# Second half of the MLP with the weight blocks stationary, evacuated as columns and transposed back to rows

## The chip, the cores and the metric

The kernel runs on one core of one Trainium2 chip. The time is device microseconds of one launch, from the chip. Everything is float32.

## What is computed

The reference is two layers over x (16 sequences of 112 rows, 512 wide) and a context (16 x 375 x 512): a cross-attention block with an MLP, then a recurrent block. Cut to what matters here:

```
# layer 0, x: (16, 112, 512), ctx: (16, 375, 512)
hidden = softmax(mask(q @ k.T * scale)) @ v @ cproj_w + cproj_b + x      # q from layer_norm(x), k, v from ctx, 16 heads
y = layer_norm(hidden, ln2_w, ln2_b)
y = gelu(y @ fc_w + fc_b, approximate=True)      # fc_w: 512 x 2048
y = y @ proj_w + proj_b                          # proj_w: 2048 x 512   <- the change
x = hidden + y
# layer 1, recurrent, 32 heads of 16:
xa = ln(x); sx = shifted(xa) - xa                # mixes, low-rank products, projections r, k, v, g
s = k v^T + w * s                                # scan over the 112 rows
x1 = x + group_norm(out) * g @ Wo.T
return x1 + sigmoid(xr2 @ Wfr.T) * (relu(xk2 @ Wfk.T)**2 @ Wfv.T)
```

## The kernel before

The 16 sequences are worked in four groups g = 0..3 of four sequences b (`GB = 4`, `T = GB * LQ = 448` columns). All engines run programs written out by hand, with semaphores between them; nothing is scheduled by a planner. For each group TensorE (PE) runs: the attention steps of its four sequences; `mlp(g)`; `border(g)`; `pre(g)` (the first mixes and projections of the recurrent layer). The recurrence of group p = g - 1 runs on VectorE (DVE), cut into `scan_unit`s of some 2 us that are laid between DVE's attention work of group g, and what is left of them is done during `mlp(g)`. After group 3 a last stage runs its scan and the second half of layer 1. "Rows" means that the 112 sequence positions lie on the partitions and the 512 channels along the free axis; "columns" means 128 channels on the partitions (four such blocks e) and 448 positions along the free axis.

`mlp(g)` takes the 2048 hidden channels in four pieces m. A piece is 16 products of `fc` (channels on the partitions, 448 positions moving, weight block stationary; ScalarE (ACT) applies gelu into `HT`, line 1150) and then 16 products of `pj` (line 533): stationary is `HT[:, c, b]` (128 x 112), moving is the weight row block `w[:, c, :]` (512 wide), and the output is rows, one PSUM bank of `SC` = (2, 3, 4, 5) for each sequence b, accumulated over all 16 blocks (m, c). With the last c of the last m the tiles `("ACC", g, b)` are closed one after another. The trace has two TensorE instructions for each of these matmuls, and one for each transpose.

PSUM has eight banks; a bank can be opened again when its last tile is freed by the engine that reads it. `WIDE` = (0, 1, 6, 7) is taken in turn by the `fc` products and, in `border`, by the transposes `pre_cols` and the products `recurrence_out`. Weights come through `ring`, two slots of 1 MB, filled by SyncE (SP) in the order of use, each when the piece before last is over.

What follows the MLP, in `border(g)`:

- DVE: `mlp_add(g, b)` (X += bank, line 1534, then the layer-norm statistics, lines 1312 and 1314), GpSimd (POOL) makes 1/std (lines 868, 871), DVE `pre_apply(g, b)` (line 1540).
- PE: for g = 0 only `pre_cols(g, 0..3)` (line 368, four transposes each), each waiting for its `pre_apply`. For g > 0: `recurrence_out` 0 and 1 (the output projection Wo of group g - 1, 8 instructions each of 512 columns, out of `C[0]`, which waits for `og_ready`), `pre_cols` 0 and 1, `recurrence_out` 2, `pre_cols` 2 and 3, `recurrence_out` 3. DVE adds each to X (line 1546).
- ACT turns the four `("LN", "pre", g, b)` tiles into `XA` (line 1057), DVE makes the shifted difference and the mixes (lines 1462 to 1457), and PE begins `pre(g)` (line 611).

`og_ready` comes at the end of a chain on DVE: scan of p done, `group_norm(p)` (its square root is on ACT, line 1167, behind gelu number (3, 0) in ACT's program), y out to DRAM and back in another layout (SP, `y_columns`), `gate(g)` (lines 1520 and 1523).

`mlp_bias(g)` (line 1528) adds `proj_b`, spread over the rows in `pb`, to X: one DVE instruction of 112 x 2048 for each group, before DVE's remaining scan units. `pb` is loaded at the start by ACT's queue (line 1026), one of 13 loads that ACT issues before its first activation; TensorE and DVE wait for 11 of them as `PARAMS`.

`C[1]` (128 x 4 x 448) is a work buffer: the scan of group p keeps its state in it (`S_mid`) and `pre(g)` its mixes.

## Time and profile before

| | |
|---|---|
| median of 3 runs | 1761.23 us (1757.83 to 1768.81) |
| the profiled execution, its time | 1756.24 us |
| its span in the trace | 1753.9 us |
| TensorE busy | 1638.1 us, 93% |
| VectorE busy | 1188.7 us, 68% |
| ScalarE busy | 657.4 us, 37% |
| GpSimd busy | 281.6 us, 16% |
| granted TensorE clock, mean | 0.975 |

The trace numbers are from one profiled execution. "Busy" counts an instruction from start to end; TensorE instructions overlap, so the pace of a stream of them is read from start to start and not from the duration of one. The chain that ended last is followed back from the last instruction; a wait is listed in square brackets behind the row that waited, with the engine and tile that ended it.

### The profile page before, as it was taken

The numbers are of one execution on the slowest core, as the hardware profiler recorded it, in microseconds if no ns is written. First come the engines' busy times: TensorE is split into PE (matmuls) and PEld (weight loads), VectorE is DVE, ScalarE is ACT, GpSimd is POOL, SyncE is SP. The second block draws the span as 40 slices with busy tenths as digits, with TensorE's granted clock in tenths as the row PEclk, the third lists the DMA queues.
The fourth block names the chain that finished last, engine by engine and source line by source line (L and its number), as shares of the span: only waits on it lengthen the run. The fifth ranks groups of instructions, "written<-read, shape, count | busy, mean of one in ns | idle before, by whom it ended". The sixth has DMA issues, their size and how long they took to land.

```text
span 1753.9 us, 21083 instructions
## 1 busy us (share of the span) xinstructions
PE 1638.1 (93%) x7912; PEld 855.8 (49%) x7912; DVE 1188.7 (68%) x1854; ACT 657.4 (37%) x1535; POOL 281.6 (16%) x377
## 2 busy tenths in 40 slices
PE   6999999799999999899999998999899898987968
PEld 3555544455555444455554445555444454433423
DVE  1233200367997995569988955799899576999741
ACT  2466420226664212246662222466431226212111
POOL 1100000123111001322110011221100132036020
PEclk9999999899999999999999999999999998999989
DMA  8001012143121124341112233510132343232221
GB/s 272 6 30 53 19 48 80 68 138 99 38 61 50 64 84 143 102 135 46 38 59 75 76 129 96 161 46 9 47 101 83 117 115 111 64 105 77 69 90 45
DMA packets 76914, 142.46 MB, mean 81 GB/s; under 512 B 16688, under 2 KB 26800, under 8 KB 76816
## 3 DMA queue, kind: packets, MB, share of 16 engines
q1 hardware_dynamic: 61664, 105.51, 18.9%
q0 software_dynamic: 11776, 31.70, 6.4%
q10 hardware_dynamic: 3376, 3.93, 0.7%
q8 instruction: 64, 1.05, 0.2%
q14 instruction: 34, 0.28, 0.1%
HBM read 117.26 MB, written 23.86 MB: 80 GB/s over the span
## 4 chain that ended last, share of the span: by engine, by line
PE 74%; DVE 16%; issue 4%; ACT 3%; ACTq 1%; DMA 1%; POOL 0%; DVEq 0%; POOLq 0%
PE bank L346 42%; PE bank L533 12%; PE bank L660 7%; PE bank L388 4%; DVE C L1399 3%; PE bank L380 3%; PE bank L400 2%; DVE sm L1336 1%; PE bank L626 1%; DVE C L1575 1%; DVE C L1391 1%; PE bank L611 1%; DVE SX L1399 1%; DVE C L1408 1%; DVE YB L1417 1%
## 5 line engine op out<-in xcount | busy, mean ns | idle before, releaser
L1399 DVE TENSOR_TENSOR_SCAN C<-XA,C 128x896 f32<-128x896 f32 x112 | 228.8, 2043 | 3.7 <-ACT XA L1091 0.5
L533 PE MATMUL bank<-ring,HT 128*112 128x512 f32 x512 | 222.3, 592 | 0.0
L1336 DVE CUSTOM_DVE_ANT_0 sm<-bank,maskb 112x375 f32<-112x375 f32 x256 | 124.3, 543 | 133.6 <-PE bank L380 133.1
L346 PE MATMUL bank<-ctx_t,Wk 128*128 128x375 f32 x512 | 195.2, 506 | 13.9 <-DMA Wk<-in_wk 12.5
L346 PE MATMUL bank<-SX,ring 128*128 128x448 f32 (+2 forms) x544 | 195.9, 519 | 4.1 <-issue 4.1
L346 PE MATMUL bank<-Wv,ctx_t 128*125 128x512 f32 x384 | 180.9, 596 | 0.4 <-ACT C L1057 0.4
L388 PEld LDWEIGHTS bank<-ident,sm 112*125 112x125 f32 x768 | 124.1, 190 | 105.6 <-ACT sm L1072 44.1
L1078 ACT ACTIVATE probT<-bank 125x336 f32<-125x336 f32 x256 | 114.3, 446 | 159.3 <-PE bank L388 157.6
L1072 ACT ACTIVATE sm<-sm,nm 112x375 f32<-112x375 f32 x256 | 153.4, 599 | 2.7 <-DVE nm L1336 2.7
L533 PEld LDWEIGHTS bank<-ring,HT 128*112 128x112 f32 x512 | 90.6, 177 | 127.2 <-issue 127.2
L346 PEld LDWEIGHTS bank<-SX,ring 128*128 128x128 f32 x544 | 100.5, 190 | 96.9 <-issue 94.0
L1150 ACT ACTIVATE HT<-bank,colt 128x448 f32<-128x448 f32 x64 | 40.5, 634 | 257.6 <-PE bank L346 257.5
L388 PE MATMUL bank<-ident,sm 112*125 112x112 f32 x768 | 125.4, 272 | 9.0 <-ACT probT L1078 8.9
L346 PEld LDWEIGHTS bank<-ctx_t,Wk 128*128 128x128 f32 x512 | 90.5, 196 | 62.2 <-issue 28.2
L1391 DVE TENSOR_TENSOR C<-VB,rkw 128x1776 f32<-128x1776 f32 x56 | 112.3, 2005 | 8.4 <-DMA VB<-v_scratch 4.1
L660 PE MATMUL bank<-C,ring 128*128 128x448 f32 x256 | 107.2, 569 | 10.3 <-DVE C L1590 7.7
L1091 ACT ACTIVATE XA<-rkw 128x896 f32<-128x896 f32 x64 | 60.9, 952 | 130.3 <-DVE C L1408 47.7
L1408 DVE TENSOR_TENSOR C<-C,rkw 128x1792 f32<-128x1792 f32 x53 | 107.3, 2025 | 1.8
L868 POOL TENSOR_SCALAR vare_ln<-mv_ln 112x1 f32<-112x1 f32 x32 | 21.9, 686 | 467.5 <-DVE mv_ln L1314 467.5
L1417 DVE TENSOR_TENSOR YB<-YB,C 128x1792 f32<-128x1792 f32 x45 | 91.0, 2022 | 1.2
L346 PEld LDWEIGHTS bank<-Wv,ctx_t 128*125 128x125 f32 x384 | 65.0, 188 | 49.4 <-issue 49.4
L1534 DVE TENSOR_TENSOR X<-bank,X 112x512 f32<-112x512 f32 x16 | 10.9, 680 | 108.8 <-PE bank L533 108.7
(181 smaller groups left out, 2317.1 us busy)
## 6 DMA issues: line engine op xcount, KB each, us to landing
ring<-in_stream SPq DMA_DIRECT2D x64, 1024.0 KB, 5.4
ctx_t<-in_ctxT SPq DMA_DIRECT2D x16, 750.0 KB, 4.7
rkw_scratch<-HT POOLq DMA_DIRECT2D x32, 224.0 KB, 4.3
rkw<-rkw_scratch POOLq DMA_DIRECT2D x24, 224.0 KB, 3.1
HT<-in_x SPq DMA_DIRECT2D x16, 224.0 KB, 5.2
X<-in_x SPq DMA_DIRECT2D x16, 224.0 KB, 5.1
rkw_scratch<-YB POOLq DMA_DIRECT2D x16, 224.0 KB, 3.1
v_scratch<-HT POOLq DMA_DIRECT2D x16, 224.0 KB, 5.6
```

The lines of the kernel that those rows point to most:

```text
L346: last_ = nc.tensor.matmul(out_ap, pairs[k][0], pairs[k][1], start=(k == 0), stop=(k == len(pairs) - 1))
L388: last_ = nc.tensor.transpose(bank[k][0:KW, c * LQ:(c + 1) * LQ], sm[0:LQ, slot, c * KW:(c + 1) * KW], ident[0:LQ, 0:LQ])
L533: last_ = nc.tensor.matmul(bank[SC[b]][0:LQ, :], HT[:, c, b * LQ:(b + 1) * LQ], w[:, c, :], start=(m == 0 and c == 0), stop=(m == 3 and c ...
L660: last_ = nc.tensor.matmul(bank[k[e]][:, 0:T], w[:, c, e * P:(e + 1) * P], mixed[at][:, c, :], start=(c == 0), stop=(c == E - 1))
L1072: nc.scalar.activation(sm[0:LQ, slot, :], sm[0:LQ, slot, :], ACT.Exp, bias=nm[:, slot:slot + 1], scale=-1.0, accum_out=den[:, n % 2, e * H ...
L1078: nc.scalar.activation(probT[:, r, :], tile(name)[0:KW, 0:KC * LQ], ACT.Copy).then_inc(freed(name), 1)
L1091: nc.scalar.activation(wrep[:, i % 2, :].rearrange("p (j t) -> p j t", j=JH), rkw[:, (i // BLOCK) % 2, i % BLOCK, 2, :].unsqueeze(1).to_br ...
L1336: nc.vector.tensor_tensor_reduce(out=sm[0:LQ, slot, :], in0=tile(name)[0:LQ, 0:LK], in1=maskb[:, n % 2, :], scale=-SCALE, scalar=3.0e38, o ...
L1391: own.step(nc.vector.tensor_tensor(S[:, :, 1:LQ], VB[:, :, 0:LQ - 1], kk[:, 0:LQ - 1].unsqueeze(1).to_broadcast([P, RS, LQ - 1]), ALU.mult))
L1399: own.step(nc.vector.tensor_tensor_scan(out=part, data0=wrep[:, i % 2, :], data1=part, initial=0.0, op0=ALU.mult, op1=ALU.add))
L1408: prod = nc.vector.tensor_tensor((S if last or i > 0 else YB)[:, :, :], S[:, :, :], r.unsqueeze(1).to_broadcast([P, RS, LQ]), ALU.mult)
L1417: nc.vector.tensor_tensor(YB[:, :, :], YB[:, :, :], S[:, :, :], ALU.add).then_inc(scan_step, 1)
```

## The change

For the `pj` pieces the operands change places. The weight block `w[:, c, e*128:(e+1)*128]` (128 x 128) is now stationary and all 448 columns of `HT[:, c, :]` move; the output is columns, one bank of `SC` for each channel block e. For m < 3 the order is c outside, e inside, as before with b. For m = 3 it is e outside and c inside, so that the four output tiles close one after another, 4 products apart. ACT evacuates each with the bias `proj_b` as a per-partition value into `C[1][:, e, :]` (new function `mlp_out`; it waits for the end of the scan of group p, since that uses `C[1]`). PE transposes each back into rows (new function `mlp_rows`: 4 sequences, each 128 x 112 stationary against a 128 x 128 identity), one e behind the products, into the four `WIDE` banks; these are the new tiles `("AT", g, b)`, and `mlp_add` reads them in place of `ACC`. `mlp_bias`, `pb` and its load are gone; `proj_b` is 4 more columns of `colt`. In `border` for g > 0 the tiles of `pre_cols` and `recurrence_out` get fixed banks in place of the turn, and `any_first` starts with `WIDE` from its first bank.

```diff
-                    for c in range(E):
-                        evacuated(pe, ("FC", g, 4 * m + c))
-                        for b in range(GB):
-                            if m == 0 and c == 0:
-                                opened(SC[b])
-                            last_ = nc.tensor.matmul(bank[SC[b]][0:LQ, :], HT[:, c, b * LQ:(b + 1) * LQ], w[:, c, :],
-                                                     start=(m == 0 and c == 0), stop=(m == 3 and c == E - 1))
-                            if m == 3 and c == E - 1:
-                                closed(last_, ("ACC", g, b), SC[b])
+                    if m < 3:
+                        for c in range(E):
+                            evacuated(pe, ("FC", g, 4 * m + c))
+                            for e in range(E):
+                                if m == 0 and c == 0:
+                                    opened(SC[e])
+                                last_ = nc.tensor.matmul(bank[SC[e]][:, 0:T], w[:, c, e * P:(e + 1) * P], HT[:, c, :],
+                                                         start=(m == 0 and c == 0), stop=False)
+                    else:
+                        for e in range(E):
+                            for c in range(E):
+                                evacuated(pe, ("FC", g, 4 * m + c))
+                                last_ = nc.tensor.matmul(bank[SC[e]][:, 0:T], w[:, c, e * P:(e + 1) * P], HT[:, c, :],
+                                                         start=False, stop=(c == E - 1))
+                            closed(last_, ("ACC", g, e), SC[e])
+                            if e > 0:
+                                mlp_rows(g, e - 1)
+                        mlp_rows(g, E - 1)
...
+            def mlp_rows(g, e):
+                evacuated(pe, ("ACC", g, e))
+                for b in range(GB):
+                    if e == 0:
+                        opened(WIDE[b])
+                    last_ = nc.tensor.transpose(bank[WIDE[b]][0:LQ, e * P:(e + 1) * P],
+                                                C[1][:, e, b * LQ:(b + 1) * LQ], ident[:, :])
+                    if e == E - 1:
+                        closed(last_, ("AT", g, b), WIDE[b])
...
             def pre_cols(g, b):
-                k = wide()
+                k = opened((SC[2], SC[3], WIDE[1], WIDE[2])[b])
             def recurrence_out(g, w, b):
-                k = wide()
+                k = opened((SC[0], SC[1], WIDE[0], WIDE[3])[b]) if g < NG else wide()
...
-            act.dma_start(pb[:, :], proj_b.partition_broadcast(LQ)).then_inc(params_in, 16)
...
+            def mlp_out(g):
+                if g > 0:
+                    act.wait_ge(scan_step, g * RS)
+                for e in range(E):
+                    name = ("ACC", g, e)
+                    ready(act, name)
+                    nc.scalar.activation(C[1][:, e, :], tile(name)[:, 0:T], ACT.Identity, bias=col("proj_b", e)
+                                         ).then_inc(freed(name), 1)
...
             def mlp_add(g, b):
-                name, rows = ("ACC", g, b), rows_of(g, b)
+                name, rows = ("AT", g, b), rows_of(g, b)
...
-                    mlp_bias(g)
```

TensorE at the end of `mlp(1)` and in `border(1)`, before (the last four of the 16 `pj` products, then the border; `ring,C0` are the products of Wo, `ident,xn` and `ident,GT` the transposes of `pre_cols`):

```order
L533 MATMUL bank2<-ring,HT 112x512
L533 MATMUL bank3<-ring,HT 112x512
L533 MATMUL bank4<-ring,HT 112x512
L533 MATMUL bank5<-ring,HT 112x512
L346 MATMUL bank1<-ring,C0 112x512 x4
L346 MATMUL bank6<-ring,C0 112x512 x4
L368 MATMUL bank7<-ident,xn 128x112 x4
L368 MATMUL bank0<-ident,xn 128x112 x4
```

The same place in the changed kernel, from the fourth of the four output tiles of the last piece on (`ident,C1` are the new transposes):

```order
L538 MATMUL bank5<-HT,ring 128x448 x4
L556 MATMUL bank0<-ident,C1 112x128
L556 MATMUL bank1<-ident,C1 112x128
L556 MATMUL bank6<-ident,C1 112x128
L556 MATMUL bank7<-ident,C1 112x128
L556 MATMUL bank0<-ident,C1 112x128
L556 MATMUL bank1<-ident,C1 112x128
L556 MATMUL bank6<-ident,C1 112x128
L556 MATMUL bank7<-ident,C1 112x128
L344 MATMUL bank2<-ring,C0 112x512 x4
L344 MATMUL bank3<-ring,C0 112x512 x4
L366 MATMUL bank4<-ident,xn 128x112 x4
```

Behind the last product stand eight transposes (four for e = 2, then four for e = 3), and only then the first product of Wo; it has moved from bank 1 to bank 2, the first `pre_cols` from bank 7 to bank 4.

ACT's queue at the start, before, from the fourth load on (the loads stand ahead of ACT's first activation):

```order
L1025 DMA Wc<-in_wc 128x4x512
L1026 DMA pb<-in_proj_b 112x512
L1027 DMA mw<-in_maa_w 128x4x160
L1028 DMA mw<-in_maa_w 128x512
L1029 DMA mw2b<-in_maa_w 128x512
```

In the changed kernel the load of `pb` is missing and the others follow in the same order.

## Rows read from the trace of the kernel before

**Rows 1.** Page: busy times; lines of the chain that ended last
```profile
PE 1638.1 (93%) x7912; PEld 855.8 (49%) x7912; DVE 1188.7 (68%) x1854; ACT 657.4 (37%) x1535; POOL 281.6 (16%) x377
PE bank L346 42%; PE bank L533 12%; PE bank L660 7%; PE bank L388 4%; DVE C L1399 3%; PE bank L380 3%; PE bank L400 2%; DVE sm L1336 1%; PE bank L626 1%; DVE C L1575 1%; DVE C L1391 1%; PE bank L611 1%; DVE SX L1399 1%; DVE C L1408 1%; DVE YB L1417 1%
```

**Rows 2.** Table by stretches: from:to and length, busy of each engine, granted clock
```profile
238.90:329.90 91.00, 90.99 (x224) 40.54 (x222) 2.38 (x5) 8.24 (x13) 0.67 (x2) 1.00 0.25 81
329.90:341.20 11.30, 3.23 (x16) 2.12 (x16) 7.58 (x17) 5.71 (x16) 5.28 (x11) 0.69 0.31 104
408.00:559.00 151.00, 149.59 (x997) 87.82 (x997) 140.98 (x234) 99.69 (x263) 31.17 (x30) 1.00 0.16 44
1113.00:1273.80 160.80, 147.20 (x960) 84.97 (x960) 146.94 (x232) 94.40 (x249) 27.31 (x26) 0.97 0.17 50
```

**Rows 3.** Chain in order of time, two pieces of mlp(0): start, length, line
```profile
252.61 12.03 PE bank L346 x32
264.63 13.73 PE bank L533 x32
```

**Rows 4.** Timeline: a pj piece begins behind an fc piece
```profile
290.23 13.90 PE L533 MATMUL bank<-ring,HT 128*112 128x512 f32 x32
290.43 0.63 ACT L1150 ACTIVATE HT<-bank,colt 128x448 f32<-128x448 f32 x1 [2.37 <-PE bank L346]
```

**Rows 5.** Timeline of TensorE in border(1): eight transposes and what follows
```profile
686.91 0.93 PE L368 MATMUL bank<-ident,xn 112*128 112x112 f32 x8
687.68 3.60 PE L346 MATMUL bank<-ring,C 128*112 128x512 f32 x8
```

**Rows 6.** Timeline of border(0), TensorE and the first DVE add
```profile
326.72 3.17 PE L533 MATMUL bank<-ring,HT 128*112 128x512 f32 x7
327.42 0.69 DVE L1534 TENSOR_TENSOR X<-bank,X 112x512 f32<-112x512 f32 x1 [105.13 <-PE bank L533]
331.06 0.61 PE L368 MATMUL bank<-ident,xn 112*128 112x112 f32 x4 [1.17 <-DVE xn L1540]
335.02 1.01 PE L368 MATMUL bank<-ident,GT 112*128 112x112 f32 x4 [1.38 <-DVE GT L1540]
341.23 4.01 PE L611 MATMUL bank<-C,mw 128*32 128x112 f32 x93 [3.89 <-DVE C L1457]
```

**Rows 7.** border(1): DVE's timeline, and the chain's piece of Wo's first products
```profile
673.89 2.03 DVE L1523 TENSOR_TENSOR C<-C,GT 128x1792 f32<-128x1792 f32 x1
680.21 6.87 PE bank L346 x16
682.72 0.52 DVE L1540 TENSOR_SCALAR xn<-X,mv_pre,rstd_pre 112x512 f32<-112x512 f32 x1
687.84 1.04 DVE L1540 TENSOR_SCALAR GT<-X,mv_pre,rstd_pre 112x512 f32<-112x512 f32 x2
```

**Rows 8.** Tile pb; then the gate of mlp(3): ACT, DVE, Wo's products, SP's loads
```profile
L1528 DVE TENSOR_TENSOR X<-X,pb x4: 2293/2293/2294, 220.0 to 1271.6; 112x2048 f32<-112x2048 f32 x4
1358.62 0.39 ACT L1167 ACTIVATE gst<-gst,epsc 128x112 f32<-128x112 f32 x1 [2.13 <-DVE gst L1448]
1372.95 2.02 DVE L1523 TENSOR_TENSOR C<-C,GT 128x1792 f32<-128x1792 f32 x1
L346 PE MATMUL bank<-ring,C x32: 591/592/595, 1377.1 to 1392.0; 128*112 128x512 f32 x32
1367.65 25.29 SPq L774 DMA_DIRECT2D ring<-in_stream  x3
ring<-in_stream SPq DMA_DIRECT2D x1, 1024.0 KB, 6.4
```

**Rows 9.** Timeline of the start: ACT's load of pb, its first activation, TensorE's wait
```profile
2.97 0.55 ACTq L1026 DMA_DIRECT2D pb<-in_proj_b  x1
19.41 1.28 ACT L1040 ACT_TABLE_LOAD   x1 [19.41 <-issue]
21.33 5.32 PE L346 MATMUL bank<-ctx_t,Wk 128*128 128x375 f32 x16 [1.45 <-ACT KT L1040]
```

More of the change, by code:

```diff
@@ L32 @@
         "r_ln1_w", "r_ln1_b", "r_ln2_w", "r_ln2_b", "maa_x",
-        "maa_0", "maa_1", "maa_2", "maa_3", "maa_4", "decay", "gn_w", "gn_b", "mix_k", "mix_r"]
+        "maa_0", "maa_1", "maa_2", "maa_3", "maa_4", "decay", "gn_w", "gn_b", "mix_k", "mix_r", "proj_b"]
 FCB = E * len(COLS)
@@ L117, in close, with build @@
         self.at[name] = (self.done, bank, self.opened[bank])
-def build(nc, x, ctxT, ctx, mask, shiftcols, cols, wq, wk, wv, wc, cproj_b, proj_b, stream,
+def build(nc, x, ctxT, ctx, mask, shiftcols, cols, wq, wk, wv, wc, cproj_b, stream,
           maa_w1, maa_w2, td_w1, td_w2, u, out):
@@ L145, in build @@
         cb = sb("cb", [LQ, D])
-        pb = sb("pb", [LQ, D])
         shc = sb("shc", [P, 2, E, B])
@@ L238, in build @@
         params_in = sem("params_in")
-        PARAMS = 11
+        PARAMS = 10
         consts_made = sem("consts_made")
@@ L329, in any_first @@
             def any_first():
-                first = turn_of["wide"] + 1
-                any_order[:] = [*SC, *(WIDE[(first + k) % 4] for k in range(4))]
+                any_order[:] = [*SC, *WIDE]
                 turn_of["any"] = -1
@@ L1280, in _ @@
                     mlp(g)
+                    mlp_out(g)
                     pre_cols(g)
@@ L1523, in gate @@
                 nc.vector.tensor_tensor(C[0][:, :, :], C[0][:, :, :], GT[:, :, :], ALU.mult).then_inc(og_ready, 1)
-            def mlp_bias(g):
-                rows = X[:, (g % 2) * GB:(g % 2 + 1) * GB, :]
-                dve.wait_ge(xn_ready["ln2"], g * GB + GB)
-                own.step(nc.vector.tensor_tensor(rows, rows, pb[:, :].unsqueeze(1).to_broadcast([LQ, GB, D]), ALU.add))
-                own.settle()
             def mlp_add(g, b):
-                name, rows = ("ACC", g, b), rows_of(g, b)
+                name, rows = ("AT", g, b), rows_of(g, b)
                 ready(dve, name)
@@ L1711 @@
             *[l1["maa_stack"][0, j] for j in range(5)], l1["time_decay"], l1["gn_w"], l1["gn_b"],
-            l1["ffn_maa_k"], l1["ffn_maa_r"], l0["fc_b"]]
+            l1["ffn_maa_k"], l1["ffn_maa_r"], l0["proj_b"], l0["fc_b"]]
     cols = np.concatenate([v.reshape(-1, P).T for v in vecs], axis=1)
@@ L1729 @@
         "wq": l0["q_w"], "wk": l0["k_w"], "wv": l0["v_w"], "wc": l0["cproj_w"],
-        "cproj_b": l0["cproj_b"], "proj_b": l0["proj_b"],
+        "cproj_b": l0["cproj_b"],
         "stream": np.stack(pieces),
```

## The prediction

> **What bounds the kernel now.** I read the page first: TensorE is busy 93% of the span, and of the chain that ended last the two matmul lines 346 and 533 alone are 54%; line 533, the second half of the MLP, is 12% of it [rows 1]. Then the table by stretches. Between 238.9 and 329.9 us (fc and pj of group 0) TensorE is busy the whole time at full granted clock, and DVE does 2.4 us of work: the MLP is TensorE's alone. Right behind it, 329.9 to 341.2 us, TensorE has 3.2 us of work in 11.3 us and waits for DVE, ACT and GpSimd in turn; this is border(0), and it is on the chain too [rows 2]. In group 3's attention (1113 to 1273.8 us) TensorE and DVE are both at 147 us of 160.8: there DVE leads [rows 2]. But its work begins only when pre(2) has produced its inputs, so a gain made upstream moves this stretch and doesn't shrink in it. The same holds for the final scan. So the end moves by the sum of what the four MLPs, the four borders behind them and the start give.
>
> **The products.** The chain has an fc piece (32 instructions of 448 columns) at 12.03 us and a pj piece (32 of 512 columns) at 13.73 us [rows 3]. After the change a pj piece has exactly the shape of an fc piece: 128 x 128 stationary, 448 moving. So 1.70 us for each of 4 pieces in 4 groups: 6.80 us a group, 27.2 us in all. The stationary block grows from 112 to 128 columns; the fc piece has that already, so 12.03 us includes it.
>
> **The transposes.** 16 a group, each 128 columns of the identity. Before, eight transposes of 112 columns go from 686.91 to 687.68 us, 0.096 us each, with products right before and behind them [rows 5]; scaled to 128 columns 0.11 us. That is 1.76 us a group, 7.0 us in all. The upper bound is the same instruction at the lower clock level: four take 1.01 us at 335.02 us against 0.61 us at 331.06 [rows 6], which with the drain taken off is about twice, 0.2 us each, 6 us more in all. Nothing suggests a price under 0.096.
>
> **The wait for the last tile.** ACT must evacuate tile e = 3 before its four transposes. The fc tiles show this latency: the next piece's first product starts at 290.23 us, ACT starts on the tile just closed at 290.43 and takes 0.63 us [rows 4]. With 0.05 us to wake TensorE that is 0.88 us, of which 0.44 us lie under the four transposes of e = 2; then 0.44 us for those of e = 3. So from the last product to the first product of Wo: 1.32 us. The other eight transposes stand between products, 0.88 us. Net for TensorE's own stream: 6.80 - 0.88 - 1.32 = 4.60 us a group.
>
> **Border(0).** Here TensorE has nothing to cover DVE's chain, and the chain's start moves the other way: before, tile b = 0 closes three tiles ahead of the end, and DVE's first add starts at 327.42, 2.30 us before the last product has issued (326.72 + 3.17 less 0.16 of drain, 329.73) [rows 6]. After, no row tile is whole until the transposes of e = 3: 0.88 + 0.11 + 0.15 (drain) = 1.14 us behind the last product. The products end 6.80 - 0.88 = 5.92 us earlier, the add is 1.14 + 2.30 = 3.44 us later against them: border(0) gains 2.48 us, not 4.60. This is the step where the change gives back most.
>
> **Borders 1 to 3.** There 6.87 us of Wo products stand before the first `pre_cols` [rows 7]. DVE's chain starts some 2.4 us later against them. Before, `pre_apply` of b = 1 is done at 683.24, 3.2 us after Wo's products began (about 680.05) and 3.7 before the transposes at 686.91; 2.4 later is still in time. `pre_apply` of b = 2, 3 is done at 688.88 [rows 7], while their transposes come at about 691.1 (687.68 + 8 x 0.43) [rows 5]; DVE's queue has slack there from waits on Wo's tiles, and by my count the second apply then ends some 1.3 us before it is needed. So nothing is lost, and the fixed banks add no wait: bank 2 to 5 are freed by ACT's four evacuations, before Wo's first product may start at all.
>
> **The gate.** Wo's products also need `og_ready`. In group 1 it comes at 675.92 [rows 7], about 4.1 us ahead of 680.05; 4.60 us would close it. But `mlp_bias`, 2.29 us of DVE ahead of the scan's rest, is gone [rows 8], and ACT reaches the square root 5.1 us (three pieces) earlier, for which DVE waited; so the gate moves by about 5 us with the products. Group 3 is tight: the square root there already waits for DVE (2.13 us), so only the 2.29 us count. og_ready goes from 1374.97 to 1372.68, the products from 1377.10 [rows 8] to 1372.50: a wait of 0.23 us. Wo's weights, issued by SP behind y at 1367.65 and 6.4 us on the way [rows 8], go the same 2.29 us earlier, to 1371.8, in time by 0.7. ACT stays blocked behind the square root until about 1358.0, and gelu 1 to 3 follow at 0.6 us each, just ahead of the products that read them. `mlp_out`'s wait for the scan's end is long over: that comes some 15 us before the gate. ACT's four evacuations lie in its idle time. Group 3 gains 4.37 us, groups 1 and 2 4.60 each.
>
> **The start.** ACT issues its 13 loads until 19.4 us, then loads its table, and only the first evacuation lets TensorE go on at 21.33, after 1.45 us of waiting [rows 9]. The issue of `pb` is 0.55 us of that, and the later issues stand in a full queue with 224 KB less ahead. Between 0 and the 1.45 us of the wait; I take 0.8.
>
> **Sum.** 2.48 + 4.60 + 4.60 + 4.37 + 0.8 = 16.85 us. Against the profiled execution, 1756.24 us: 1739.4. That execution was 5 us under the median of the three runs, 1761.23, whose range is 11 us; against that: 1744.4. I predict 1742.5, between the two.
>
> **The rivals.**
>
> A, the gain is smaller because it is taken off the path. (1) The transposes cost twice, 6 us more: a gain of 11. (2) The gate doesn't move with the products: in each of three groups Wo then starts when it starts now less what bias gives, 2.3 us instead of 4.6: 7 us less, a gain of 10. Either gives about 1749. For it speaks the tight gate in group 3; against it that DVE's idle time before the square root in groups 1 and 2 is itself due to TensorE.
>
> The Trainium skill, "TensorE: Matmul & The Clock Gate", part 4, gives about 275 ns for a 128 x 128 transpose in a kernel's context, bf16. By that the 64 new ones are 17.6 us and the change would gain about 6 us. The eight transposes that take 0.77 us in this trace speak against it as a pace; it would be a latency.
>
> B, slower than before: the clock. If TensorE fell to its lower level (1.2 GHz) at the run of eight transposes with a wait in it, and stayed there over the border, the 32 instructions of Wo (13.7 us at full clock) would take 13.7 us more, in three groups 41 us: about 1780. It is slower than before from two of the three borders on. In this trace the clock fell only in border(0), mean 0.69, after TensorE had been idle more than half of 5 us, and was 1.00 in the attention of group 1, which is full of short transposes [rows 2]. The new wait is 0.44 us. The same page, part 4, says that transposes don't engage the full clock; the attention stretch speaks against that here.
>
> C, more than I count: ACT's queue at the start frees TensorE by the full 1.45 us, and border stretches at the lower clock get shorter. Another 2 us, 1740.5.
>
> **The numbers.** My forecast with C: 0.78. A: 0.18. B: 0.04. 1% of 1761.23 is 17.6 us, about what a measurement of this kernel can tell from no change, and my sum is 16.85: it lies on that bound, and chance decides most. The median of three before lies above its profiled execution, which tilts it a little to faster. Faster by over 1%: 0.50; within 1%: 0.46; slower: 0.04, which is B. The range: 1734 (C, with a median as low as the profiled execution) to 1752 (A, with the spread of medians).
>
> **What would show it.** In the changed profile: 12.03 us a pj piece for m < 3; the last product to Wo's first 1.3 us; new transposes at 0.11 us; the first add of border(0) at about 324.9 less what the start gave; the stretch from the first product of pj (0) to Wo shorter by 4.6 us in groups 1 to 3, with at most some tenths waited for line 1523 in group 3; granted clock 1.00 in borders 1 to 3; TensorE's first wait for ACT at 0.7 us. It is wrong if the transposes are slower than 0.15 us, if `pre_cols` waits for `pre_apply` in groups 1 to 3, or if stretches outside MLP and border change length by more than a microsecond in sum.

## The result and the profile after

The changed kernel takes 1737.49 us (median of four runs, 1736.41 to 1739.64); the kernel before, measured again beside it, 1762.68 (1757.83 to 1768.81). The ratio is 0.986, with an interval of 0.984 to 0.988: faster by 1.4%. I had forecast 1742.5, in a range of 1734 to 1752. Run a second time, the changed kernel took 1739.02 us, ratio 0.985 (0.983 to 0.988). Its profiled execution is one of 1739.64 us with a span of 1736.7.

Line numbers are a little different in the new kernel: 344 is the old 346, pj is 532 (m < 3) and 538 (m = 3) instead of 533, the transposes back are 556, the first products of `pre` are 629 instead of 611. First the page's busy times and the lines of the chain that ended last (answer to [rows 1]). TensorE has 16 us less to do, and stays 93% busy: it is the bound as before.

```profile
PE 1621.9 (93%) x7976; PEld 870.2 (50%) x7976; DVE 1178.6 (68%) x1850; ACT 666.3 (38%) x1551; POOL 281.0 (16%) x377
PE bank L344 40%; PE bank L678 8%; PE bank L532 6%; DVE C L1426 5%; PE bank L386 4%; PE bank L378 3%; PE bank L538 2%; PE bank L398 2%; DVE C L1435 2%; DVE YB L1444 2%; DVE sm L1363 1%; DVE C L1596 1%; DVE C L1418 1%; PE bank L644 1%; PE bank L629 1%
```

Pieces of the chain in mlp(0) (start, length, line): a pj piece now costs what an fc piece costs, as against [rows 3]. The third row is half a piece, the part of m = 3 up to the first transposes.

```profile
239.63 12.03 PE bank L532 x32
251.65 12.03 PE bank L344 x32
311.79 6.01 PE bank L538 x16
```

The table by stretches, with the columns of [rows 2]: MLP of group 0 from pj (0), then border(0), then the first part of border(1). TensorE fills the MLP, and the granted clock is full (1.00, the level of 2.4 GHz) there and in border(1).

```profile
239.50:325.40 85.90, 85.63 (x237) 43.59 (x235) 0.00 (x0) 10.76 (x17) 0.00 (x0) 1.00 0.26 86
325.40:339.58 14.18, 4.28 (x20) 2.81 (x21) 9.98 (x21) 5.69 (x16) 5.93 (x12) 0.68 0.27 83
677.80:694.60 16.80, 15.46 (x50) 6.97 (x48) 11.91 (x24) 5.58 (x16) 5.22 (x11) 1.00 0.33 107
```

Since the granted clock differs a little from one execution to the next, spans alone don't say where the time went. So I cut every trace at TensorE's own milestones: the first pj product of group g ("pj"), and the first product of `pre(g)` (the row that answers to the last of [rows 6]). Lengths in us; "before again" and "after again" are the two kernels unchanged, run and profiled a second time.

| stretch | before | after | before again | after again |
|---|---|---|---|---|
| start to pj(0) | 238.71 | 239.46 | 240.16 | 241.31 |
| pj(0) to pre(0) | 102.52 | 100.12 | 102.52 | 100.12 |
| pre(0) to pj(1) | 247.80 | 251.80 | 247.81 | 248.28 |
| pj(1) to pre(1) | 107.84 | 103.26 | 107.84 | 103.26 |
| pre(1) to pj(2) | 249.71 | 247.57 | 249.48 | 246.90 |
| pj(2) to pre(2) | 107.84 | 103.26 | 107.84 | 103.26 |
| pre(2) to pj(3) | 231.66 | 229.68 | 231.93 | 229.64 |
| pj(3) to pre(3) | 107.84 | 104.17 | 107.83 | 104.33 |
| pre(3) to the end | 360.00 | 357.38 | 363.28 | 359.49 |

The four changed stretches repeat to 0.2 us and give 2.40 + 4.58 + 4.58 + 3.67 = 15.23 us. The others should be equal, and aren't: they differ by between -2.6 and +4.0 us in the first pair, and between -3.8 and +1.2 in the second. The two spans differ by 17.2 and 22.1 us.

### The profile page after: what moved, and what is told of

It reads as the page before. It is cut to its first block, busy times and chain, and to the rows that moved or that the text cites. A ratio compares the mean times of both kernels' runs of the same rounds, so it can differ in the third digit from the quotient of the medians.

```text
span 1736.7 us, 21228 instructions
## 1 busy us (share of the span) xinstructions
PE 1621.9 (93%) x7976; PEld 870.2 (50%) x7976; DVE 1178.6 (68%) x1850; ACT 666.3 (38%) x1551; POOL 281.0 (16%) x377
## 3 DMA queue, kind: packets, MB, share of 16 engines
q8 instruction: 64, 1.05, 0.3%
## 4 chain that ended last, share of the span: by engine, by line
PE 69%; DVE 21%; issue 5%; ACT 3%; ACTq 1%; DMA 1%; POOL 0%; SPq 0%; DVEq 0%; POOLq 0%
PE bank L344 40%; PE bank L678 8%; PE bank L532 6%; DVE C L1426 5%; PE bank L386 4%; PE bank L378 3%; PE bank L538 2%; PE bank L398 2%; DVE C L1435 2%; DVE YB L1444 2%; DVE sm L1363 1%; DVE C L1596 1%; DVE C L1418 1%; PE bank L644 1%; PE bank L629 1%
## 5 line engine op out<-in xcount | busy, mean ns | idle before, releaser
L532 PE MATMUL bank<-HT,ring 128*128 128x448 f32 x384 | 146.3, 539 | 0.0
L532 PEld LDWEIGHTS bank<-HT,ring 128*128 128x128 f32 x384 | 73.0, 190 | 71.4 <-issue 71.4
```

What stands on the lines that cost most here:

```text
L532: last_ = nc.tensor.matmul(bank[SC[e]][:, 0:T], w[:, c, e * P:(e + 1) * P], HT[:, c, :], start=(m == 0 and c == 0), stop=False)
```

## Experiments

Two theories stood against the rest. Mine: a change of this kind is worth its terms on TensorE's stream (products, transposes, one evacuation's wait). The rivals: transposes cost their recorded duration or pull down the clock; the bias instruction that left DVE brings the gain; and, for what lies outside the MLP, that it is the random clock, against something the change moved.

**The two kernels, unchanged, side by side** (no edit).

> The kernel before once more with a profile, beside the others of this call. Its first profiled execution took 1756.24 us, 5 to 7 us under its medians. Theory 1 (the difference is clock and start, outside MLP and border): MLP and border repeat (102.5 us in group 0 from the first pj product to pre's first, 107.84 in groups 1 to 3), and the spare microseconds stand in the stretches outside with a lower granted clock. Theory 2 (the profiled execution was typical and the medians of before are high for another reason): the new profile is again within 1 us of 1753.9.

> The changed kernel once more, beside the others of this call. The stretches fixed by the program (first pj product to the first product of pre) should repeat to 0.05 us: 99.95, 103.09, 103.10 and 104.17 us for groups 0 to 3. Theory 1 (the 7 us between the change in medians and the change in spans, 24.5 against 17.2, come from stretches outside MLP and border in which the granted clock falls at other moments): the stretches outside differ between two profiles of one kernel by microseconds of either sign, and the granted clock of these stretches with them. Theory 2 (the change moves work outside MLP and border for good): they repeat to some tenths.

Measured: 1761.56 us for the kernel before (0.999, 0.998 to 1.001) and 1739.02 for the changed one. The table has their stretches. The MLP and border stretches are the same in both pairs, so they are the change's; so are three of the others, by sign: pre(1) to pj(2), pre(2) to pj(3) and pre(3) to the end are shorter by 1.98 to 3.79 us in both pairs. That needed a cause of its own (below). The two traces of the kernel before differ by 4.8 us, nearly all of it ahead of pj(0) and behind pre(3); I had expected lower granted clocks there, but the longer one has the higher mean clock (0.976 against 0.975), so this difference stays open.

**Every transpose back twice.**

```diff
-                    last_ = nc.tensor.transpose(bank[WIDE[b]][0:LQ, e * P:(e + 1) * P], ...
+                    for again in range(2):
+                        last_ = nc.tensor.transpose(bank[WIDE[b]][0:LQ, e * P:(e + 1) * P], ...
```

> Each of the 64 new transposes is issued twice. Theory (0.109 us each, those of e = 2 lie under the wait for ACT as far as it goes, 0.44 us): each MLP is 12 x 0.109 longer where nothing covers (e = 0, 1 and 3) and the four more of e = 2 fill the wait of 0.44 us, so 1.31 us a group from the first pj product to the first product of Wo, 5.2 us in all; in group 3, where Wo waits 0.7 us for its weights, 0.6. Rival (a transpose costs about 275 ns on the path, the Trainium skill's figure in TensorE: Matmul & The Clock Gate, part 4): 3.3 us a group and more. Rival on the clock: the granted clock in borders 1 to 3 falls below 1.00 with 20 transposes in a row.

Measured: 1739.62 us (0.986, 0.983 to 0.989); pj to Wo 87.75 us in groups 1 and 2 (86.44 without), so 1.31 more, and 0.45 more in group 3, where I had expected 0.6. The median doesn't show the 5.2 us that I expected in all: it lies 2.1 and 0.6 us above the two medians of the changed kernel, and its four runs are spread over 7.9 us (1735.03 to 1742.92). Only the stretches show the price. Sixteen records of it in a row, from the timeline of border(1), and the group by lines (min, median and max duration in ns):

```profile
678.46 1.97 PE L557 MATMUL bank<-ident,C 128*112 128x128 f32 x16
680.27 4.03 PE L344 MATMUL bank<-ring,C 128*112 128x512 f32 x9
L557 PE MATMUL bank<-ident,C x128: 272/273/322, 317.9 to 1364.4; 128*112 128x128 f32 x128
```

Sixteen take 1.81 us, 0.11 each, and the record of one says 272 ns. So the recorded duration is how long one takes from entering to leaving, and the next enters after 0.11: a sum over durations would have been 2.5 times too high. The granted clock stayed at 1.00 in borders 1 to 3. The Trainium skill, "TensorE: Matmul & The Clock Gate", part 4, gives about 275 ns for a 128 x 128 transpose in bf16 within a kernel, and says that transposes don't bring the full clock; its figure agrees with the duration here (273 ns, in float32) and not with the pace, and its warning had no effect in a border that is mostly products.

**Transposes all at the end, and a simpler order of products.** `tail` does the four rounds of transposes only after the last product of m = 3. `couter` does that and also runs piece m = 3 in the order of the others.

```diff
 (tail)
                             closed(last_, ("ACC", g, e), SC[e])
-                            if e > 0:
-                                mlp_rows(g, e - 1)
-                        mlp_rows(g, E - 1)
+                        for e in range(E):
+                            mlp_rows(g, e)
 (couter, besides)
-                    if m < 3:
...
-                    else:
+                    for c in range(E):
+                        evacuated(pe, ("FC", g, 4 * m + c))
                         for e in range(E):
...
+                                                     start=(m == 0 and c == 0), stop=(m == 3 and c == E - 1))
+                            if m == 3 and c == E - 1:
+                                closed(last_, ("ACC", g, e), SC[e])
```

> The changed kernel with all 16 transposes of a group behind the last product. Theory: the last tile's evacuation (0.88 us) is then covered by twelve transposes (1.31 us) and not by four, TensorE's wait of 0.29 to 0.44 us goes: 0.44 us a group less up to the first product of Wo, so 99.5 us in group 0 and 102.65 in groups 1 and 2, 104.17 unchanged in group 3, where weights and gate bind; 1.3 us in all, too little for the medians. Rival: sixteen transposes in a row cost more each than four between products (0.11), or take the granted clock down behind them; then groups 1 and 2 are above 103.1 us.

> tail with c outside and e inside for the last piece too (the same loop as for the first three), so that the four column tiles close 0.75 us apart at the end and not 3.0. Theory: ACT's evacuations (0.63 us each) keep pace with tiles 0.75 us apart, and the sixteen transposes start before the last tile is needed: 99.6, 102.76, 102.76 us from the first pj product to pre's first in groups 0 to 2, as in tail to 0.1 us. The e order of the last piece is then without effect once the transposes are at the end. Rival: TensorE waits for the first tiles, and it is longer by up to 0.6 us a group.

Measured: `tail` 1732.99 us (0.982, 0.980 to 0.985), `couter` 1732.13 us (0.982, 0.980 to 0.985). pj to Wo is 85.93 in both, in groups 1 and 2, 0.51 less than in the changed kernel. The timeline of `tail` in border(1):

```profile
670.77 1.91 PE L555 MATMUL bank<-ident,C 128*112 128x128 f32 x16
672.52 7.03 PE L344 MATMUL bank<-ring,C 128*112 128x512 f32 x16
```

Sixteen transposes in 1.75 us without a gap: ACT's evacuation of tile 3 lies under the twelve transposes of tiles 0 to 2. The order c or e outermost makes no difference, so the code of the change that turned it for m = 3 isn't needed. In group 3 they gain little or nothing (87.33 and 87.06 against 87.30): Wo's first product waits there 1.2 and 1.0 us, until DVE's multiplication ends. 0.5 us in each of three groups is not the 4.5 to 5.4 us by which their medians lie under 1737.49. In the two traces much of the rest is clock: it stayed at 1.00 from 54 to 74 us, where the changed kernel's fell to 0.71, and start to pj(0) took 236.3 and 236.1 us against 239.5. But all eight runs of the two (1734.91 at most) lie below the eight of the changed kernel (1734.93 at least), and why the clock should favour them isn't shown.

**Only the operands changed, no way back.** The tiles of 448 columns are added to 448 columns of the rows as they are, without ACT's evacuation, `mlp_out` or transposes; the bias and the way back to rows are left out. A first version, `products`, took the turn-taking banks in border, and kept the changed bank order of `pre`; the second put that order back.

```diff
 (products; the loops of the products as in couter, without mlp_rows)
-                    mlp_out(g)
...
-                k = opened((SC[2], SC[3], WIDE[1], WIDE[2])[b])
+                k = wide()
...
-                k = opened((SC[0], SC[1], WIDE[0], WIDE[3])[b]) if g < NG else wide()
+                k = wide()
...
-                name, rows = ("AT", g, b), rows_of(g, b)
+                name, rows = ("ACC", g, b), rows_of(g, b)
 (products2, besides)
-                any_order[:] = [*SC, *WIDE]
+                first = turn_of["wide"] + 1
+                any_order[:] = [*SC, *(WIDE[(first + k) % 4] for k in range(4))]
```

> The changed operands of the products alone: 448 columns moving, but c outside and e inside for all four pieces, no evacuation into C[1], no transposes; DVE adds the column tiles to X as they are, so that proj_b and the way back to rows are left out. Theory: against the kernel before, each pj piece 12.03 instead of 13.73 us; from the first pj product to the first product of Wo 6.80 us shorter in groups 1 and 2 (103.1 becomes about 100.9), in group 0 border and MLP 6.5 us shorter (about 95.9 instead of 102.35 us); in group 3 the gate stands at the same place, so no shorter than the changed kernel's 104.17 us by more than 0.1 us. Span about 8 us under the changed kernel's, apart from what the clock does outside. Rival (the gate or pre_cols take the gain): groups 1 and 2 stay above 102 us.

> As products (operands changed alone, proj_b and the way back to rows left out), but with the order of banks in pre as in the kernel before: any_first begins behind the bank that the turn has reached. In products the fifth tile of pre's first product stood on bank 0, which held the last Wo tile; TensorE waited 4.98 us there for DVE's add. Theory: from Wo's first product to pre's first 16.83 us again in groups 1 and 2 (20.4 in products), so 101.0 us from the first pj product; group 3 at 104.3 (gate); group 0 unchanged at 95.7. Rival: the wait in products came from something else and stays.

Measured: `products` 1741.34 us (0.986, 0.982 to 0.990), `products2` 1733.99 (0.984, 0.982 to 0.987). pj to Wo is 84.19 in both, 6.82 less than 91.01: the term for the operands alone (6.80) to 0.02. But Wo to `pre` took 20.4 us in `products`, where 16.8 is usual. The first line is its timeline in border(1):

```profile
686.15 6.07 PE L620 MATMUL bank<-C,mw 128*32 128x112 f32 x128 [4.98 <-DVE X L1558]
685.19 0.68 DVE L1558 TENSOR_TENSOR X<-bank,X 112x512 f32<-112x512 f32 x1
```

`pre`'s fifth tile fell on the bank that held the last Wo tile, and TensorE stood 5 us until DVE had read it. I hadn't foreseen that wait; with the order of banks put back, pj to pre is 101.02, as expected. It also shows that the banks of border and the order in which `pre` opens them belong together: the change turned both, and to turn one alone costs 3.6 us a border (104.6 against 101.0). Group 3 came out at 102.17 instead of 104.3: DVE's multiplication ended 85.2 us behind the first pj product, where the changed kernel has 87.2. The stretch pre(2) to pj(3), in which DVE scans, had been 2.1 us longer (231.7 against 229.7).

**The bias back on DVE.** `mlp_bias` as before, at its old place, with `cb` as the operand (2.29 us of DVE in each group).

```diff
                     y_apply(n)
+                    mlp_bias(g)
...
+                own.step(nc.vector.tensor_tensor(rows, rows, cb[:, :].unsqueeze(1).to_broadcast([LQ, GB, D]), ALU.add))
```

> The changed kernel with one DVE instruction of 112 x 2048 back in the place of mlp_bias, adding cb (already on chip) in place of pb, so that the output has a wrong bias and the load at the start stays away. Theory: DVE's chain to og_ready in group 3 is 2.29 us later and Wo waits that much longer, 89.6 us from first pj product to Wo instead of 87.3; groups 1 and 2 have room of 5.1 us and stay at 86.44; group 0 stays. Rival A2 (the gate binds in groups 1 and 2 as well): these move too.

Measured: 1740.65 us (0.988, 0.987 to 0.990); pj to pre 103.27 in groups 1 and 2, unchanged, and 105.85 in group 3, 1.7 more than 104.17. So what left DVE brought nothing where TensorE sets the end, and 1.6 to 1.7 us in the one group in which the gate is tight. The full 2.29 don't arrive, because DVE's wait for y took up part of it: DVE's last write of y came 2.1 us later, but it then waited 9.06 us for y where it had waited 9.61, so the multiplication ended 1.6 us later (88.8 against 87.2 us behind the first pj product; in the kernel before, 88.9). The chain in `gate`'s timeline of group 3:

```profile
1359.16 1.78 DVE L1547 TENSOR_SCALAR C<-C,colt 128x448 f32<-128x448 f32 x4 [9.06 <-DMA C<-y_scratch]
1360.97 2.03 DVE L1550 TENSOR_TENSOR C<-C,GT 128x1792 f32<-128x1792 f32 x1
1363.16 3.26 PE L344 MATMUL bank<-ring,C 128*112 128x512 f32 x7 [0.21 <-DMA ring<-in_stream]
```

**The load of `pb` back.**

```diff
+        pb = sb("pb", [LQ, D])
...
-        PARAMS = 10
+        PARAMS = 11
...
+            act.dma_start(pb[:, :], proj_b.partition_broadcast(LQ)).then_inc(params_in, 16)
```

> The changed kernel with the load of pb kept at its old place in ACT's queue and nothing reading it. Theory: ACT's first activation comes 0.8 us later again (19.4 instead of 18.6 us), and TensorE's third key product at 21.3 instead of 20.54 us; TensorE starts its first product at 12.5 instead of 11.3 us; all stretches of MLP and border as in the changed kernel. Rival C (the start gives nothing or the full 1.45 us).

Measured: 1738.65 us (0.987, 0.985 to 0.989), so nothing that a time can show against 1737.49 and 1739.02. In the trace, ACT's table load begins at 19.42 and the third key product at 21.34 us, as before ([rows 9]: 19.41 and 21.33), against 18.62 and 20.54 without the load. TensorE's own first product was expected at 12.5 us again and came at 11.11 (11.26 in the changed kernel), so that part was a miss. The load of `pb` doesn't set it: the second trace of the kernel before, which has the load, begins at 11.20.

```profile
19.42 1.28 ACT L1059 ACT_TABLE_LOAD   x1 [19.42 <-PE bank L345]
21.34 1.85 PE L345 MATMUL bank<-ctx_t,Wk 128*128 128x375 f32 x5 [2.14 <-ACT KT L1059]
```

This run also had no wait at Wo in group 3 (86.44, as in groups 1 and 2): its attention of group 3 was 3.8 us longer, at a mean granted clock of 0.96 against 0.97, and y went out 1.7 us earlier against the first pj product. A longer attention leaves DVE more time ahead of the gate, and its length differs from one execution to the next. That isn't the whole rule: `couter`, whose attention of group 3 was 2.2 us shorter, waited no longer for it.

**The kernel before, its instructions moved.** Sixteen transposes that nobody reads, ahead of the first fc product of each group: 32 instructions, weight loads included, and 1.75 us each. It tells whether the shorter stretches behind the borders come from where the instructions lie.

```diff
                     evacuated(pe, ("TY", g * GB + b))
+                for again in range(16):
+                    nc.tensor.transpose(bank[first][:, 0:P], ident[:, :], ident[:, :])
```

> The kernel before with 16 more transposes of the identity in each group, at the start of mlp(g), into a bank that the next product overwrites: TensorE's program is as much longer before each border as in the changed kernel, and nothing else is touched. Before, TensorE stops for 1.86, 1.26 and 1.46 us in the middle of pre's first product (line 611) in borders 1 to 3, with nothing that it waits for; in the changed kernel these stops are gone, and in products2, which has the changed products but no transposes, they are there (1.67, 1.12, 1.82). Theory F (the stops come when TensorE's next 16 KB of instructions are late, and their place in the program decides): no stop of over 0.4 us in line 611 in groups 1 to 3; from pre's first product to the next pj product about 2 us less the 1.75 us that the added transposes take (they lie in this stretch): 249.7 becomes 249.5, 231.7 becomes 231.5; pj to pre unchanged at 107.84. Theory G (the changed banks of pre took the stops away): they stay at 1.3 to 1.9 us, and the stretches are 251.4 and 233.4 us.

Measured: 1769.96 us (1.003, 1.001 to 1.005), some 6 us more (2 to 10), where 64 transposes take 7.0. pj to pre stayed at 107.84. Theory F, that the place in the program decides, holds for groups 1 and 3 (no stop; pre(1) to pj(2) 249.18 us, expected 249.5) and missed group 2, where a stop of 2.63 us was left (236.11 us, expected 231.5). G falls, since the banks are those of the kernel before. What follows from its trace stands in the last section.

**A version that should beat all.** `tail`, and the gate by blocks: each e of `C[0]` is multiplied at once and raises `og_ready`, Wo's first tile waits block by block, and SP issues Wo's weights ahead of y's last two loads.

```diff
+                    for e in range(E):
+                        own.step(nc.vector.tensor_scalar(C[0][:, e, :], ...))
+                        gated(e)
...
+                        pe.wait_ge(og_ready, (g - 1) * E + c + 1)
...
+                    if b == 2 and between is not None:
+                        piece(between)
```

> tail with two changes for group 3, where Wo's first product waited for its weights (0.7 us in the changed kernel, 1.2 in tail) and for the gate: SP issues the load of Wo's weights between the second and third of the four loads of y and not behind the fourth, and the gate multiplies and releases each of the four blocks apart, with Wo's first tile waiting for one block at a time. Theory: weights 1.0 us earlier; group 3 from first pj product to Wo's first at 86.0 to 86.5 us instead of 87.33, groups 0 to 2 as in tail (85.94). Too little for the medians: within 0.2% of tail (1733). Rival: the loads of y and of the weights share the queues, and y's last block comes as much later as the weights come earlier: 87.3 or more.

Measured: 1737.20 us (0.985, 0.982 to 0.988). pj to pre is 106.15 in group 3, 1.9 more than in `tail`:

```profile
1359.45 0.51 DVE L1560 TENSOR_SCALAR C<-C,colt 128x448 f32<-128x448 f32 x1 [13.16 <-DMA C<-y_scratch]
1360.77 7.70 PE L344 MATMUL bank<-ring,C 128*112 128x512 f32 x16 [1.78 <-DVE C L1557]
```

The 1 MB of weights in front held up y's last blocks: DVE waited 13.2 us for y where it waited 9.6 before. The rival came true. The weights hadn't been the last thing to come in `tail` either: they landed 87.09 us behind the first pj product, and DVE's multiplication ended at 87.23. `couter` has the lowest median, 1732.13 us, and less code than the change; from `tail` (1732.99) the times can't tell it.

## Why the prediction was right, and where it wasn't

**The products: right.** 12.03 us a piece; 6.82 us a group alone, in `products2`.

**The transposes and the wait: right.** The timeline of border(0):

```profile
317.64 0.60 PE L556 MATMUL bank<-ident,C 128*112 128x128 f32 x4
318.07 3.17 PE L538 MATMUL bank<-HT,ring 128*128 128x448 f32 x8
324.53 0.60 PE L556 MATMUL bank<-ident,C 128*112 128x128 f32 x4
324.73 0.63 ACT L1188 ACTIVATE C<-bank,colt 128x448 f32<-128x448 f32 x1 [2.81 <-PE bank L538]
325.42 0.65 PE L556 MATMUL bank<-ident,C 128*112 128x128 f32 x4 [0.29 <-ACT C L1188]
325.78 0.69 DVE L1555 TENSOR_TENSOR X<-bank,X 112x512 f32<-112x512 f32 x1 [105.06 <-PE bank L556]
339.58 2.79 PE L629 MATMUL bank<-C,mw 128*32 128x112 f32 x53 [3.89 <-DVE C L1484]
```

Four transposes take 0.43 us from their first to the next product (317.64 to 318.07), 0.108 each; I had 0.11 from [rows 5]. Those of e = 3 begin 0.89 us after those of e = 2 (I: 0.88), because ACT begins at 324.73 and takes 0.63. In border(1) the last product to Wo's first is 1.37 us (I: 1.32).

**Border(0): right.** DVE's first add starts 86.3 us behind the first pj product (325.78 less 239.46), where it was 88.7 (327.42 less 238.71); the stretch gained 2.40 us, of 2.48 forecast.

**Borders 1 and 2: right.** 4.58 of 4.60, and no wait of TensorE for `pre_apply`:

```profile
676.45 0.60 PE L556 MATMUL bank<-ident,C 128*112 128x128 f32 x4
677.34 0.65 PE L556 MATMUL bank<-ident,C 128*112 128x128 f32 x4 [0.29 <-ACT C L1188]
677.82 7.03 PE L344 MATMUL bank<-ring,C 128*112 128x512 f32 x16
682.75 0.52 DVE L1561 TENSOR_SCALAR xn<-X,mv_pre,rstd_pre 112x512 f32<-112x512 f32 x1
684.69 0.93 PE L366 MATMUL bank<-ident,xn 112*128 112x112 f32 x8
686.14 1.16 DVE L1561 TENSOR_SCALAR GT<-X,mv_pre,rstd_pre 112x512 f32<-112x512 f32 x2
694.64 4.30 PE L629 MATMUL bank<-C,mw 128*32 128x112 f32 x160 [1.38 <-DVE C L1484]
```

`pre_apply` of b = 0 and 1 is over by 683.3, and its transposes begin at 684.69; the apply of b = 2 and 3 is done at 687.3, where the products after 685.46 last until 688.9. `pre`'s wait of 1.38 us was there before. The gate moved too: DVE's multiplication ended at 672.70 us, 5.1 ahead of Wo, and 4.4 ahead in group 2 (before, 4.1 and 4.2).

**Group 3: the mechanism right, a term too small.** I had 4.37 and it is 3.67: Wo waited 0.70 us, where I had 0.23. The last row is from the kernel before:

```profile
1354.55 7.26 DMA ring<-in_stream
1358.51 1.78 DVE L1547 TENSOR_SCALAR C<-C,colt 128x448 f32<-128x448 f32 x4 [9.61 <-DMA C<-y_scratch]
1360.33 2.03 DVE L1550 TENSOR_TENSOR C<-C,GT 128x1792 f32<-128x1792 f32 x1
1362.45 7.09 PE L344 MATMUL bank<-ring,C 128*112 128x512 f32 x16 [0.70 <-DMA ring<-in_stream]
1371.13 1.78 DVE L1520 TENSOR_SCALAR C<-C,colt 128x448 f32<-128x448 f32 x4 [9.18 <-DMA C<-y_scratch]
```

The profile puts Wo's wait down to its weights, but these had landed at 1361.81 (1354.55 + 7.26), and DVE's multiplication ended at 1362.36, 0.09 us ahead of Wo's first product. So the gate came last; `tail`, `couter` and the second trace of the changed kernel have the same order, with Wo 0.10 us behind the multiplication. The term that was too small is the gate's: I let `og_ready` move by the whole 2.29 us of the bias, with y's trip unchanged. DVE's last write of y came 2.12 us earlier against the first pj product, and its wait for y grew from 9.18 to 9.61, so the multiplication was 1.7 us earlier and not 2.29. The weights were mis-sized too: in time by 0.7 us at the 6.4 that this load took before [rows 8], and at 7.26 some 0.2 us too late for TensorE, hidden behind the gate.

**The start: right at its first step, not shown at the end.** The third key product came 0.79 us earlier, of 0.8, and in the second pair of traces 0.26 (20.83 against 21.09). TensorE's wait for ACT was to shrink to 0.7 us and is 1.40, since TensorE's first product also came earlier (11.26 us, before 12.47). And start to pj(0) took longer with the change in both pairs, by 0.75 and 1.15 us, so no run shows that the 0.8 reaches the end.

```profile
18.62 1.28 ACT L1057 ACT_TABLE_LOAD   x1 [18.62 <-issue]
```

**The step that failed** is the one I put as "the end moves by the sum of what the four MLPs, the four borders behind them and the start give". My last sentence had the rest changing by less than a microsecond in sum; it changed by -2.0 us in the first pair of traces and by -7.0 in the second, with single stretches off by up to 4 us in both directions. The sum against the profiled execution, 1739.4, met 1739.64 partly because errors cancelled: in that pair the changed stretches gave 15.23 of 16.05, TensorE's stops behind borders 1 to 3 another 4.6 that I hadn't seen, and the clock took about 3.3 in pre(0) to pj(1). So that the sum met it was in part luck, and the medians, which fell by 25.2 and not by 16.85, put the forecast 5 us too high. The second pair of traces, whose spans stand closer to the medians of their runs, differs by 22.1 us: 15.1 in the changed stretches, 4.9 in stops, and 2.1 for all else. The medians of that pair differ by 22.5, those of the first by 25.2; the 2.7 between them stay open, and are within the spread of the runs.

**The rivals.** A fell in both forms: transposes at 0.108 us, and the gate moved with the products in groups 1 and 2 (0.7 us of it came true, in group 3). B fell: granted clock 1.00 in borders 1 to 3, even with twice the transposes. One premise of mine against it was wrong, though: the clock hadn't fallen only in border(0). In the kernel before it was at 0.68 from 62 to 66 us too, and 0.97 in group 3's attention [rows 2]. C, more than counted, came about, but not by its own mechanism.

## What to carry to other kernels

Swapping the operands to move 448 columns instead of 512 takes 1.70 us off each piece of 16 products, and the way back costs 16 x 0.109 = 1.75 us however many pieces accumulate: with the four pieces of this kernel the gain is 4.6 to 5.1 us a group; with one piece it would be a small loss, by an estimate from these two numbers that no run tried. Put the transposes behind the last product, so that the first tiles' cover the last tile's evacuation, and look at which bank the next stage opens first. Compare traces stage by stage before you believe a difference of spans, since the stages that nothing touched moved by up to 4 us here.

## What the runs showed of the hardware

**TensorE can run out of instructions.** Before, in borders 1 to 3 TensorE stops in the middle of `pre`'s first products, with nothing that it waits for. The timeline of the kernel before:

```profile
696.87 3.90 PE L611 MATMUL bank<-C,mw 128*32 128x112 f32 x143 [1.39 <-DVE C L1457]
702.63 0.67 PE L611 MATMUL bank<-C,mw 128*32 128x112 f32 x17 [1.86 <-issue]
1059.97 0.39 PE L611 MATMUL bank<-C,mw 128*32 128x112 f32 x6 [1.26 <-issue]
1399.30 0.59 PE L611 MATMUL bank<-C,mw 128*32 128x112 f32 x16 [1.46 <-issue]
```

Here 160 matmuls with as many weight loads enter in some 4.1 us, 13 ns each. The profile page's section of DMA queues has one called "instruction", with 64 packets and 1.05 MB in the execution, 16 KB each; in the stretch 700.0 to 700.5 us of the kernel before it is this row (packets, MB, share):

```profile
q8 instruction: 1, 0.02, 12.1%
```

TensorE goes on about 2.2 us behind the start of that packet in all three cases that I looked at (700.38 and 702.63; 1057.79 and 1059.97; in `double` 1384.70 and 1386.95). The stops summed to 4.6 and 4.9 us in the two traces of the kernel before, and were 0 in both of the changed kernel, in `tail`, `couter`, `best`, `gate` and `pbload`; `products2`, with its other count of instructions, had them in all three borders (1.67, 1.12, 1.82), and `double` in group 3 (1.73), with one of 0.34 in group 2 just behind the burst. `products` had none, but there TensorE had stood 5 us ahead of the burst. `shift` moved the instructions of the kernel before and nothing else:

```profile
707.60 4.30 PE L613 MATMUL bank<-C,mw 128*32 128x112 f32 x160 [1.39 <-DVE C L1459]
1064.62 3.13 PE L613 MATMUL bank<-C,mw 128*32 128x112 f32 x106 [1.39 <-DVE C L1459]
1070.38 2.84 PE L613 MATMUL bank<-C,mw 128*32 128x112 f32 x54 [2.63 <-issue]
```

None in groups 1 and 3, and one of 2.63 us in group 2, at another place of the burst. That a stop depends on where the burst lies in the program is shown; my expectation of none over 0.4 us was a miss.

Two things that I overlooked make it firmer. Number TensorE's records in the trace (weight loads, matmuls and waits on semaphores) in order: all eleven stops in this burst stand at 7106, 10945, 14529 or 14785, each 193 or 194 past a multiple of 256, whatever place of the burst that is. `shift`, with 96 instructions added by then, stopped at the same 10945 as the kernel before, at the 213th record of the burst in place of the 309th. And wherever it stopped, no packet of that queue had started in the 38 us ahead of the burst, and the next came 3.2 to 3.5 us into it; in the 25 bursts of groups 1 to 3 that ran through (those of `products` apart), one had started 5.6 to 24 us ahead. In the changed kernel's border(1) that is the packet at 687.8 us, ahead of the burst at 694.64. This fits packets that bring TensorE's instructions in blocks of 256, and a stop when the next block is fetched only after the burst has begun; it is still read from place and time, since no row names what a packet holds. Part of this change's gain is that luck, and an edit anywhere ahead can give it back. The stops are 4.6 of the 6.7 us by which the three stretches behind borders 1 to 3 are shorter in the first pair, and 4.9 of 8.7 in the second; the rest of it stays open.

The Trainium skill, "Runtime: NRT & Kernel Launch", section "Instruction fetch mechanics", says that instructions come in blocks of 16 KiB, 256 of them, and that fetching is mostly hidden behind the pace of issue. The size agrees with the packets here, and the 256 with the distance of the stops; "hidden" doesn't hold in a burst at 13 ns an instruction.

**The clock can fall after a short wait in one execution and not in the next.** Attention of group 1, timeline of the changed kernel and table by stretches (granted clock third from the end), then the same from its second trace:

```profile
407.52 2.74 PE L378 MATMUL bank<-KT,qT 32*112 32x375 f32 x8 [0.83 <-DVE nm L1363]
413.45 2.64 PE L344 MATMUL bank<-ctx_t,Wk 128*128 128x375 f32 x4
410.00:412.00 2.00, 2.00 (x4) 1.18 (x4) 1.85 (x6) 0.23 (x2) 0.00 (x0) 0.50 1.05 323
412.00:414.00 2.00, 2.00 (x6) 1.30 (x5) 1.34 (x2) 0.31 (x1) 0.00 (x0) 0.50 0.36 94
```

```profile
409.18 2.19 PE L378 MATMUL bank<-KT,qT 32*112 32x375 f32 x8 [0.83 <-DVE nm L1363]
412.98 1.44 PE L344 MATMUL bank<-ctx_t,Wk 128*128 128x375 f32 x4
410.00:412.00 2.00, 2.00 (x9) 1.02 (x7) 2.00 (x9) 1.88 (x8) 0.82 (x2) 1.00 0.97 340
```

It is one kernel, with the same instructions ahead and the same wait of 0.83 us. In the one execution the clock went to 0.50, the level of 1.2 GHz, for 6.8 us, and in the other it stayed at 1.00. From the eight products to the second group of three at line 386 it is 8.40 us against 5.08, 3.3 lost, which is most of the 3.5 us by which the two differ in pre(0) to pj(1). The two traces of the kernel before lost nothing in this place. Whether the change makes the loss likelier stays open: of the eight traces with the new products and transposes, seven lost 3.4 or 6.8 us of full clock here, but so did `shift`, which has neither the new products nor the way back.
